# Feed-forward chunks and down jobs of the last batch in other slots of a hand-ordered transformer block

## What is computed

```
x = L0_attn_x
xn = _layernorm(x, axis=-1)
x = x + _L0_attn_ref(xn, w_qkv, b_qkv, w_out, b_out) + _L0_ffn_ref(xn, gate_w, up_w, down_w, gate_s, up_s, down_s)
...
scores = einsum('bhqd,bhkd->bhqk', q, k) / sqrt(32) + causal
out = einsum('bhqk,bhkd->bhqd', softmax(scores), v)
...
hdn = silu((xf @ gate_w.T) * gate_s) * ((xf @ up_w.T) * up_s)
out = (hdn @ down_w.T) * down_s
```

## Time and profile before

| | us |
|---|---|
| median of 3 executions | 1979.67 |
| lowest, highest | 1974.18, 1979.82 |
| the profiled execution, its own time | 1980.58 |
| its span in the trace | 1978.8 |

### The profile page before, as it was taken

The page is one execution under the profiler, slowest core; times in us unless marked ns, Lnnn a source line. Parts: engine busy times, 40 slices in busy tenths (PEclk is TensorE's granted clock), DMA queues, the critical chain, the costliest instruction groups (busy, mean ns, idle before and its releaser), DMA issues.

```text
span 1978.8 us, 43848 instructions
## 1 busy us (share of the span) xinstructions
PE 1877.3 (95%) x14978; PEld 1218.0 (62%) x14978; DVE 1688.3 (85%) x5012; ACT 1352.3 (68%) x3784; POOL 1137.9 (58%) x1620
## 2 busy tenths in 40 slices
PE   6699999999999999999999999999999999999997
PEld 3456575666656666566666756666566666756663
DVE  4878889988898888989889898888989788898885
ACT  3767676867767676676767767676676666767673
POOL 3565656647466475655757575465655556465352
PEclk9899999999999999999999999999999999999998
DMA  7987978888698787978788697886968778797674
GB/s 210 238 149 140 187 139 174 157 155 176 126 194 140 157 169 142 185 133 175 159 150 185 133 192 120 159 155 129 184 126 170 135 141 172 135 180 128 126 152 92
DMA packets 819094, 310.24 MB, mean 157 GB/s; under 512 B 756465, under 2 KB 789233, under 8 KB 818865
## 3 DMA queue, kind: packets, MB, share of 16 engines
q1 hardware_dynamic: 801504, 250.49, 69.6%
q0 software_dynamic: 17360, 56.90, 10.3%
HBM read 55.59 MB, written 16.78 MB: 37 GB/s over the span
## 4 chain that ended last, share of the span: by engine, by line
PE 49%; DVE 31%; SPq 6%; DMA 5%; ACT 5%; issue 3%; POOL 1%; DVEq 0%; ACTq 0%; POOLq 0%
PE bank L268 49%; DVE phl L556 8%; DVE bank L546 6%; DMA pt<-phl 4%; SPq L887 4%; ACT phl L456 3%; DVE fh L568 3%; DVE small L537 2%; DVE ft L564 2%; DVE res L580 2%; DVE xhl L691 2%; DVE xs L528 1%; SPq L894 1%; ACT bank L464 1%; DVE small L518 1%
## 5 line engine op out<-in xcount | busy, mean ns | idle before, releaser
L456 ACT ACTIVATE phl<-bank,small 128x512 f16<-128x512 f32 (+3 forms) x1024 | 500.0, 531 | 277.0 <-DVE small L537 211.0
L464 ACT ACTIVATE bank<-bank,small 128x512 f32<-128x512 f32 (+3 forms) x1024 | 513.6, 502 | 183.2 <-DVE small L546 176.6
L556 DVE SCALAR_TENSOR_TENSOR phl<-bank,small,phl 128x512 f16<-128x512 f32 (+3 forms) x1024 | 524.6, 543 | 72.8 <-ACT phl L456 68.9
L546 DVE CUSTOM_DVE_ANT_0 bank<-bank,mask 128x512 f32<-128x512 f32 (+3 forms) x1024 | 485.2, 504 | 92.1 <-PE bank L268 91.8
L752 POOL TENSOR_SCALAR ht<-fh 128x256 f16<-128x256 f32 x352 | 143.3, 407 | 463.8 <-DVE fh L568 463.2
L268 PE MATMUL bank<-xnT,wg 128*128 128x256 f16 x2816 | 368.5, 274 | 10.0 <-DVE fh L568 10.0
L268 PE MATMUL bank<-xnT,wu 128*128 128x256 f16 x2816 | 366.8, 273 | 0.0
L268 PE MATMUL bank<-xnT,wqkv 128*128 128x512 f16 x1536 | 354.8, 381 | 4.5 <-DVE vv L574 4.5
L268 PE MATMUL bank<-wd,ht 128*128 128x512 f16 x1408 | 318.6, 383 | 0.2 <-issue 0.2
L268 PEld LDWEIGHTS bank<-xnT,wg 128*128 128x128 f16 x2816 | 263.5, 98 | 73.6 <-issue 8.3
L268 PEld LDWEIGHTS bank<-xnT,wu 128*128 128x128 f16 x2816 | 276.6, 98 | 33.0
(11 more groups left out here) (103 smaller groups left out, 2069.3 us busy)
## 6 DMA issues: line engine op xcount, KB each, us to landing
stk<-qkp SPq DMA_DIRECT2D x768, 64.0 KB, 2.2
res<-in_x_dram POOLq DMA_DIRECT2D x64, 256.0 KB, 4.8
xin<-in_x_dram POOLq DMA_DIRECT2D x60, 256.0 KB, 4.6
out_dram<-res POOLq DMA_DIRECT2D x60, 256.0 KB, 3.8
pt<-phl SPq DMA_TRANSPOSE x512, 4.3
xin<-in_gate_dram POOLq DMA_DIRECT2D x11, 256.0 KB, 3.7
xin<-in_up_dram POOLq DMA_DIRECT2D x11, 256.0 KB, 3.7
xin<-in_down_dram POOLq DMA_DIRECT2D x11, 256.0 KB, 3.6
```

Of the source, the lines that this page charges most:

```text
L456: i = eng.activation(phl[qt][:, j % 2, 0], pb[:, off:off + W], ACT.Copy, scale=st_r[:, c:c + 1])
L464: i = eng.activation(pb[:, off:off + W], pb[:, off:off + W], ACT.Exp, bias=st_m[:, c:c + 1], scale=-1.0, accum_out=st_s[:, c:c + 1])
L546: i = eng.tensor_tensor_reduce(out=bk[:, off:off + W], in0=bk[:, off:off + W], in1=mask[:, 512 - W:512], scale=-(32.0 ** -0.5) / (QS * QS) ...
L556: i = eng.scalar_tensor_tensor(phl[qt][:, j % 2, 1], pb[:, off:off + W], st_r[:, c:c + 1], phl[qt][:, j % 2, 0], ALU.mult, ALU.subtract)
```

## The change

A second table, `F_LAST`, holds for the last four groups: 3 chunks in group 1 (2, 4, 7), 4 in group 2 (0, 2, 4, 7), 6 in group 3 (0, 1, 3, 5, 7, 9) and 6 in group 4 (0, 2, 3, 5, 6, 8), again 19. And in the last batch d0 and d1 go from units 19 and 21 to 23 and 25, d2 and d3 from units 37 and 39 to turns 40 and 41. No instruction is added or taken away, and nothing ahead of the last batch differs.

```
     F_WIN = ((2, 2, 4, 5), (0, 2, 4, 5, 8), (0, 2, 4, 5, 7, 8), (0, 0, 2, 3, 4, 5, 8))
+    F_LAST = ((2, 4, 7), (0, 2, 4, 7), (0, 1, 3, 5, 7, 9), (0, 2, 3, 5, 6, 8))
...
-        for where in (2, 4, 5, 7, 8, 9) if G == 0 else F_WIN[G % 4]:
+        for where in (2, 4, 5, 7, 8, 9) if G == 0 else (F_WIN if G < NGRP - 4 else F_LAST)[G % 4]:
...
-        for t, k in enumerate((19, 21, 37, 39)):
+        for t, k in enumerate((19, 21, 37, 39) if b < B - 1 else (23, 25, 40, 41)):
             d_at[40 * b + k] = (b, t)
```

## The result

| | before | changed |
|---|---|---|
| median, us | 1979.67 | 1995.92 |
| lowest, highest of 5 executions, us | 1974.18, 1984.68 | 1991.63, 1997.70 |
| the profiled execution, us (span) | 1980.58 (1978.8) | 1995.92 (1994.1) |
| engine PE, DVE busy | 95%, 85% | 94%, 85% |

The changed kernel is slower by a ratio of 1.0065, with a 95% interval of 1.0037 to 1.0093. On 1979.67 that is 13 us, between 7 and 18. I had forecast slower by 7.3; the point of the ratio is 1992.5, near the upper end of my range, and the median itself lies 3 us above that end.

What follows compares the result with a forecast made beforehand. DVE's list was taken to bound the last batch until unit 39's maximum, PE's after it. Terms -1.5 - 0.9 + 1.7 - 2.9 + 8.3 + 2.6 = +7.3 us gave 1987.0 us, range 1980.5 to 1993.

Steps and rivals of the forecast that it cites:

- What bounds: Last batch: DVE's list sets the pace until unit 39's maximum at 1951.30, PE's list after it.
- rival 1: PE, not DVE, limits groups 1 and 2, which then give 5.6 us; 1983.8 us in all; chance 0.23.
- Groups 1 and 2: Last batch, first twenty units: each group loses a chunk on DVE; minus 1.5 us and minus 0.9 us.
- the chunk is minus 0.92: In group 2, one chunk fewer takes 0.92 us off DVE; d0's going gives nothing.
- Group 3: Units 20 to 29: DVE waits 2.2 and 3.5 us behind d0 and d1, has one chunk less; plus 1.7 us.
- Group 4: Up to unit 39's maximum: d2's 3.46 us wait and a scaling go, DVE does two more chunks; minus 2.9 us.
- the end: From unit 39's maximum to the last `av`: 19.2 us instead of 10.87, PE alone setting the time; plus 8.3 us.
- the clock: Behind a PE gap of some 4 us, the early output products run at the lower clock; plus 2.6 us.
- Rival 2: Levelling works, no slower: PE's lead covers both blocks of group 3; 1976.2 us; chance 0.08.
- Rival 3: PE cold through the last two groups: d0 at low clock, group 4 at its upper bound; +12.3, 1992.0 us; chance 0.13.
- My own signs: Last batch, expected in the trace: shorter early groups, earlier unit 39 maximum, PE idling 4 us in group 2, 19 to 22 us afterwards.
- The total: Sum of all terms, all in the last batch: +7.3 us, giving 1987.0 us by the median.

Runs made afterwards that it cites:

- the filled gap: Changed kernel plus 12 extra PE products in turn 39, ahead of the early output products; last batch 144.67 us, ratio 1.0051 against the kernel before.

## Why the prediction was right, and where it missed

**What bounds.** That DVE's list paces the units held in group 2: moving d0 out of it freed 4.75 us of PE and no time (28.36 in the half with d0 and d1 alone). There rival 1, PE as the limit, is refuted. For group 1 no run took work from PE alone. With DVE's tests out of it PE was busy for 29.24 of 29.24 us, so PE lay at most 1 us below DVE there. Both groups together gave 0.6 us, not the 5.6 of rival 1.

**Groups 1 and 2** were sized wrongly. The step that failed is "the chunk is minus 0.92": the two groups gave 0.5 and 0.1 where the sum had 1.5 and 0.9. A unit without its chunk can leave DVE waiting for ACT. In unit 16 the chunk went and this wait stood ahead of `low`:

```profile
1894.85 0.88 DVE L557 SCALAR_TENSOR_TENSOR phl<-bank,small,phl 128x256 f16<-128x256 f32 x2 [0.59 <-ACT phl L457]
```

From its maximum to the next unit's took 2.20 us instead of 2.38; in unit 18, which got a chunk, 3.49 instead of 2.70. In groups 1 and 2 the two units that got a chunk (8 and 18) grew by 0.79 us each, and the four that lost one (3, 6, 16 and 19) shrank by 0.57, 0.48, 0.18 and 0.68. In group 1 part of the gain also went into DVE's operation behind the reciprocals (L538), which took 0.56 and 0.42 us in units 3 and 5 instead of 0.19 and 0.17; what held it is open. The sum also gave half of 1.1 us of waits back in group 1, but of DVE's waits there one of 0.30 us for PE went and one of 0.31 for ACT came.

**Group 3** grew by 3.2 and not 1.7. The two waits were right, 2.40 and 2.98 us against 2.2 and 3.5. What I left out are again the small waits: behind the two for PE they come to 2.0 us in the group, 0.48 and 0.48 for ACT in the rows above among them, where the kernel before had 0.6. The chunk that leaves the group took only 0.45 us off DVE's busy time, since other operations grew.

**Group 4** was right (minus 3.2 against minus 2.9), and by its parts too: d2 and d3 gone alone gave 4.0 us where the sum had 4.06, and the two more chunks then cost 0.9 (21.16 to 22.03) where it had 1.1. So was **the end**: 10.2 us more against 8.3 and 2.6 for the clock. The wait for the last chunk was 1.97 us (1.8 in the sum). The clock was priced too high: the gap was 2.58 us and not 4, and the first nine products took 3.69 us, 1.7 more than 1.98 and not 2.6. The clock's price is shown as a cause by the filled gap, minus 1.77. The Trainium skill, page "TensorE: Matmul & The Clock Gate", section "Why this matters for your kernels", advises against idle gaps between bursts of matmuls, and speaks of longer gaps than these. The traces agree with the advice even for waits of 2.58 and 2.88 us: products that nobody reads won 1.77 and 1.6 us there.

**Rival 2** (no slower) did not win, because DVE did wait behind both blocks of group 3, 5.4 us in all, and because the end took its price. The Trainium skill, page "Perfetto Trace Analysis", section "Optimization Strategy", says only that interleaving regimes may help; here it did not.

**Rival 3** (PE at the lower clock through the last two groups) forecast 1992.0, nearer to the measured 1992.5 than my own 1987.0, but not for its reason: d0 ran at the higher clock in the changed kernel (its 22 products took 4.9 us), and group 4 came out at my own figure, not at the bound.

**My own signs.** Several failed, and the total hides it. Unit 39's maximum was to come 2 to 5 us earlier (3.6 in the sum) and came 0.5 earlier, so nearly the whole gain is missing; groups 1 and 2 were to be 1 to 3 us shorter and were 0.6; PE was to idle at least 4 us in group 2, else I would be wrong, and idled 3.88, with a busy share of 86% and not near 80. The waits behind both blocks, the 19 to 22 us at the end (21.02) and the lower clock at its start did show. The range held because the end, the largest term by far, was sized well.

**The total** of the last batch was +9.9 against +7.3: groups 1 to 3 missed by 3.3, the rest gave 0.7 back. The other 3 us of the measured 13 are in none of these stages. Between the two traces, 5.4 of the 15.3 us lie ahead of the last batch, where the order is the same. The start of the last batch scatters by 12 us between traces, and the interval of the ratio reaches down to 7 us. The five executions of the changed kernel are not the whole of it: in all ten versions that leave the code ahead of the last batch alone, against different executions of the kernel before, the ratio's point lies above what the stages give, by 0.6 to 3.9 us. The cause is open. My range had no term for it, and that the ratio's point fell inside the range, 0.5 us from its end, is in part luck.

## What to carry to other kernels

An engine that is 99% busy need not be the limit. Take its work away in one place, see whether the next stage starts earlier, and look at the chain of waits before work is moved away from it. Work that is put behind the last step of a pipeline costs its full length there, while the place that it left gives back only what no other engine was waiting to take. When a step is taken out of a unit, ask which wait it had covered, since that wait comes back. When PE must idle ahead of a burst that nothing hides, harmless products in the gap can pay for themselves.

## What the runs showed that I had not expected

- With the same order, groups 1 and 2 repeat within 0.05 us between traces (but for one), and what scatters later starts in two kinds of place. Where PE comes back from a gap, the granted clock is at one or the other level by chance: behind the same wait of 2.27 us d0 took 6.61 us in one trace and 4.92 in another, and d2 took between 6.60 and 7.71. And where ACT waits for a transposing transfer, a unit can be longer by 1.2 us.
- Three limits lay within 2 us in group 2. PE was busy for 28.08 of 28.30 us, and 4.75 us of its work taken away gave nothing; DVE's work taken away gave 0.4 in the kernel before and 0.9 in the changed one; six transfers of SP's list moved back in that one went with 1.2 more, to 26.16.
- From unit 39's maximum to the last `av` there is a floor of 10.45 to 10.5 us, with PE idle for 4.5 us ahead of that `av`. It is SP's issue of the last three transposing transfers (1.3 to 1.6 us each, one behind the other) and the landing of the third, 3.1 us.
